# First loads of a second loop, spread over the last eight groups of the loop before it

## What is computed

```python
xn = _layernorm(x, gamma, beta)
x_inner, z = jnp.split(xn @ W_in, 2, axis=-1)
xc = depthwise_conv(x_inner, conv_w, taps=4, causal) + conv_b
x_conv = silu(xc)
xp = x_conv @ W_x                    # B (16), C (16), one delta
delta = softplus(xp[:, :, -1:])
y = selective_scan(x_conv, -exp(A_log), B, C, delta)
y = (y + x_conv * D_skip) * silu(z)
x = _layernorm(x + (y @ W_out + residual))
```

## Time and profile before

| what | us |
|---|---|
| runs, median (lowest to highest of 3) | 1719.43 (1718.05 to 1721.29) |
| the profiled execution, its own time | 1721.67 |
| its span from first to last instruction | 1719.8 |
| first loop and what leads to it, to the end of PE's projections | 0 to 245.6 |
| between the loops and first two steps | 245.6 to 291.1 |
| second loop | 291.1 to 491.5 |
| attention and experts | 491.5 to 1719.8 |
| PE busy over the whole span | 1648.0 |

### The profile page before, as it was taken

One profiled execution on the slowest core, in us unless ns is written; L12 is line 12 of the kernel. 1 busy time (PEld: TensorE's weight loads), 2 busy tenths in 40 slices (PEclk: granted clock), 3 DMA queues, 4 the chain that ended last, 5 costly groups with the idle time before them and its releaser, 6 DMA issues.

```text
span 1719.8 us, 38082 instructions
## 1 busy us (share of the span) xinstructions
PE 1648.0 (96%) x11304; PEld 1492.5 (87%) x11305; DVE 1303.9 (76%) x2688; ACT 947.1 (55%) x1643; POOL 871.4 (51%) x770
## 2 busy tenths in 40 slices
PE   7999986999998999999999998999999999999994
PEld 6777765988987888888888878999999999999994
DVE  6888867888885776776776778767777777777774
ACT  6888876777843334334334345555555565555552
POOL 2111125888972345345345353555666666666664
PEclk9999988999998999999999999999999999999998
DMA  4555556899964343342342344334555455445454
GB/s 151 191 190 190 190 194 203 247 262 265 266 229 140 112 135 103 111 136 97 115 136 100 111 151 122 62 61 98 104 98 106 101 99 114 97 94 117 94 104 106
DMA packets 149263, 240.79 MB, mean 140 GB/s; under 512 B 40960, under 2 KB 104640, under 8 KB 141008
## 3 DMA queue, kind: packets, MB, share of 16 engines
q1 hardware_dynamic: 122608, 203.58, 38.1%
q0 software_dynamic: 26592, 36.46, 12.1%
HBM read 132.30 MB, written 107.68 MB: 140 GB/s over the span
## 4 chain that ended last, share of the span: by engine, by line
PE 62%; DMA 3%; DVE 2%; issue 1%; POOL 1%; ACT 0%; SPq 0%; DVEq 0%; ACTq 0%; POOLq 0%
PE block_banks L3094 22%; PE block_banks L3144 11%; PE block_banks L2976 5%; PE block_banks L2985 5%; PE block_banks L2899 4%; PE block_banks L2998 4%; PE block_banks L2920 2%; PE block_banks L3087 2%; PE block_banks L2939 2%; PE block_banks L2931 2%; PE block_banks L2887 1%; PE block_banks L2956 1%; DMA more<-back_y,back_token 1%; DMA attention_x<-x 1%; POOL sorted L2185 0%
## 5 line engine op out<-in xcount | busy, mean ns | idle before, releaser
L3094 PE MATMUL block_banks<-back_xe_T,back_w_split 128*128 128x256 f32 x3408 | 437.3, 285 | 2.4 <-DVE back_xe_T L2768 1.5
L3094 PEld LDWEIGHTS block_banks<-back_xe_T,back_w_split 128*128 128x128 f32 x3408 | 418.1, 192 | 2.8 <-issue 1.7
L2349 ACT ACTIVATE back_w_split<-back_w_gu 128x1024 fp32r x142 | 149.8, 1056 | 233.3 <-PE block_banks L3094 231.2
L3144 PE MATMUL block_banks<-back_w_down,back_he_T 128*128 x1680 | 213.1, 283 | 1.0 <-DVE back_w_down L2425 1.0
L3144 PEld LDWEIGHTS block_banks<-back_w_down,back_he_T 128*128 128x128 f32 x1680 | 206.6, 192 | 1.2 <-issue 1.2
L2748 DVE TENSOR_TENSOR back_w_split<-back_w_gu,back_w_split 128x1024 fp32r<-128x1024 f32 x142 | 179.6, 1265 | 36.9 <-ACT back_w_split L2349 36.7
L2185 POOL DMA_INDIRECT sorted<-back_x,back_slot x128 | 129.9, 1015 | 127.7 <-DVE back_slot L2571 80.5
L1582 PE MATMUL block_banks<-front_xn_T,front_w_in_parts 128*128 128x512 f32 x768 | 184.8, 395 | 2.4 <-DVE front_xn_T L1353 1.1
L1582 PEld LDWEIGHTS block_banks<-front_xn_T,front_w_in_parts 128*128 128x128 f32 x768 | 141.4, 188 | 39.2 <-DVE front_conv L1346 7.5
L2221 POOL DMA_INDIRECT acc<-back_y,back_token x71 | 112.3, 1581 | 120.5 <-DVE back_y L2787 116.2
L1346 DVE SCALAR_TENSOR_TENSOR front_conv<-block_banks,front_conv_wb,front_conv 128x508 f32<-128x508 f32 (+2 forms) x192 | 140.7, 740 | 33.0 <-ACT front_conv L1130 28.3
(11 more groups left out here) (290 smaller groups left out, 3492.0 us busy)
## 6 DMA issues: line engine op xcount, KB each, us to landing
back_xe<-sorted SPq DMA_DIRECT2D x72, 272.0 KB, 2.8
gate_T<-front_gate_T SPq DMA_DIRECT2D x16, 1024.0 KB, 4.8
xc_T<-front_xc_T SPq DMA_DIRECT2D x16, 1024.0 KB, 5.8
front_xc_in<-xc_T SPq DMA_DIRECT2D x16, 1024.0 KB, 7.4
front_gate_in<-gate_T SPq DMA_DIRECT2D x16, 1024.0 KB, 6.3
front_c_rep<-c_parts SPq DMA_DIRECT2D x128, 64.0 KB, 5.5
front_rows_in<-in_x SPq DMA_DIRECT2D x16, 512.0 KB, 8.2
x<-front_x SPq DMA_DIRECT2D x16, 512.0 KB, 3.1
```

The source lines that it names most:

```text
L2349: nc.scalar.activation(w_split[:, r, 0, m].unsqueeze(1), w_gu[:, bass.ds(e, 1), m], ACT.Copy).then_inc(w_high_ready, 1)
L3094: op = nc.tensor.matmul(dst[:, part, c % 2 * WINDOW:(c % 2 + 1) * WINDOW], w_split[:, r, w_part, m, k * D_FF + c * P:k * D_FF + (c + 1) * ...
L3144: op = nc.tensor.matmul(ps_y[:, s, 0:D_MODEL], he_T[:, r, h_part, k, seq(s)], w_down[:, bass.ds(e, 1), w_part, k], start=(n == 0), stop=(n ...
```

## The change

`load_first` goes. Its 50 DMAs are issued in pieces by `load_sooner(g)`, which SP calls behind the `gate_T` store of each group from 8 to 15. To let it know g as a number, SP's loop runs over groups 2 to 7 only and the last eight groups are written out. Loads of groups 0 and 1 and the data they move stay the same. The wait for all stores becomes a wait for all but the last pair's, and the full wait comes in step 1, ahead of the store of `delta`. No other engine's code changes.

```diff
-            def load_reps(g, u):
-                for c in range(ENDS):
+            def load_reps(g, u, ends=range(ENDS)):
+                for c in ends:
...
-            def load_first(u):
-                if u == 0:
-                    sp.wait_ge(cleared, 3)
-                    sp.wait_ge(chain_step, W_STEPS)
-                sp.wait_ge(xp_stored[u], 16 + 32)
-                load_reps(u, u)
-                load_c(u, u)
-                sp.wait_ge(xc_stored[u], 32)
-                load_xc(u, u)
-                sp.wait_ge(gate_stored[u], 32)
-                load_gate(u, u)
-                load_rows(u, u)
+            def load_sooner(g):
+                if g == GROUPS - 8:
+                    sp.wait_ge(xc_stored[0], 32)
+                    load_xc(0, 0)
+                if g == GROUPS - 7:
+                    sp.wait_ge(gate_stored[0], 32)
+                    load_gate(0, 0)
+                if g == GROUPS - 6:
+                    load_rows(0, 0)
+                    sp.wait_ge(chain_step, W_STEPS)
+                    sp.wait_ge(xp_stored[0], 16 + 32)
+                    load_c(0, 0)
+                if g == GROUPS - 5:
+                    sp.wait_ge(cleared, 3)
+                    load_reps(0, 0, range(ENDS // 2))
+                if g == GROUPS - 4:
+                    load_reps(0, 0, range(ENDS // 2, ENDS))
+                    sp.wait_ge(xc_stored[1], 32)
+                    load_xc(1, 1)
+                if g == GROUPS - 3:
+                    sp.wait_ge(gate_stored[1], 32)
+                    load_gate(1, 1)
+                    load_rows(1, 1)
+                if g == GROUPS - 2:
+                    sp.wait_ge(xp_stored[1], 16 + 32)
+                    load_c(1, 1)
+                if g == GROUPS - 1:
+                    load_reps(1, 1)
...
-                    if last:
-                        load_first(u)
                     sp.wait_ge(gate_T_ready, KI * (g + 1) + 2)
                     sp.dma_start(d["gate_T"][g], gate_T[:, u]).then_inc(gate_stored[u], 16)
-
-            in_pairs(sp, body)
+                    if isinstance(g, int):
+                        load_sooner(g)
+
+            def groups_stored(pairs):
+                for stored, each in ((xc_stored, 16), (gate_stored, 16), (xp_stored, 32)):
+                    for u in range(2):
+                        sp.wait_ge(stored[u], each * pairs + 16)
+
+            body(0, False)
+            with sp.Fori(1, PAIRS - 4) as pair:
+                body(pair, False)
+            for pair in range(PAIRS - 4, PAIRS):
+                body(pair, pair == PAIRS - 1)
             store_xc(GROUPS - 1, 1)
             store_xp(GROUPS - 1, 1)
-            for stored, each in ((xc_stored, 16), (gate_stored, 16), (xp_stored, 32)):
-                for u in range(2):
-                    sp.wait_ge(stored[u], each * PAIRS + 16)
+            groups_stored(PAIRS - 1)
...
                 if is_at(k, 1):
+                    groups_stored(PAIRS)
                     sp.wait_ge(delta_rows_ready, 1)
```

## The result

The changed kernel takes 1725.9 us, median of 8 runs (1722.15 to 1727.64), against 1718.9 us for the kernel before, also 8 runs. The ratio is 1.0037, 95% interval 1.0028 to 1.0046, so about +6.4 us (+4.8 to +7.9); the two medians as they stand lie 7.0 us apart. One run of the kernel before, 3287.91 us, was disturbed and is left out of the ratio. The profiled execution took 1725.78 us, with a span of 1723.9. The forecast was 1719.5, range 1715.5 to 1723.0: the result is outside, on the slow side.

The account below looks back on a forecast made before the run. PE was taken to bound both loops, nearly always busy, with 6.4 us of waits for `xc_in` the most to win. -2.6 + 2.7 = +0.1 us on the median 1719.43 gave 1719.5, range 1715.5 to 1723.0.

Parts of the forecast that it names:

- the sum of what it costs in the first loop: First loop: moved DMAs delay `x_rows` and so PE, 0.7 + 2.0 = +2.7 us, from 1.2 to 4.4.
- g = 8 and 9: First loop: one megabyte each ahead of `x_rows`, 3.4 us, loss 0.37 us each; bounds 0 and 0.94 each.
- g = 10: First loop: nine DMAs ahead, `x_rows` out at 4.7 us, landed at 8.3: covered, 0.2 as upper bound.
- g = 12: First loop: eight small DMAs and the xc load ahead, `x_rows` landed at 11.4 us: loss 2.0, bounds 1.2 to 2.3.
- rival 2: First loop: hole at g = 12 lowers PE's clock, 1.8 us; with dearer queued loads +3.6, 1723.0; chance 0.15.
- g = 11 and 13 to 15: First loop: six small DMAs at the first of these are covered; later stores in the rest cost nothing.
- The term of the gain: Second loop: SP starts sooner, so PE waits less for `xc_in`: -2.6 us, bounds 1.1 and 6.4.
- The wait of 1.11 us: PE's wait for `xc_in` at 291.11, to go since xc of group 2 is issued 8.5 us sooner.
- The lead of 2.6 us at xc of group 4: Second loop: that load goes out at 308.4 instead of 310.99, and SP stays ahead by 2.6 us.
- the waits of 6.4 us to be won: PE's waits for `xc_in`, 5.3 us in the second loop and 1.11 before: the most earlier loads could give back.
- Rival 1: First loop's loads covered, only g = 12 costs, 1.2 us; larger lead, 1716.6, or 1714.2 with all waits won; chance 0.25.
- Rival 3: Second loop: lead lost to transfers ahead in the queue, only 1.11 us come; sum +1.6, 1721.0; chance 0.13.

Follow-up runs that it names:

- e4: Kernel after, with the eight `c_rep` loads of g = 10 cut from 64 KB to 4 KB each, full ones loaded at g = 13; 1721.78 us, one run.
- e7: Kernel after, with only the xc load of g = 12 moved behind the next `x_rows` load; 1724.69 us, one run.
- e11: Kernel after, with the pieces of groups 8 to 11 put behind the `x_rows` load, that of group 12 left ahead; 1728.68 us, one run.
- e5: Kernel before, unchanged, as its second profile; the kernel before against itself measured 0.9997, not assigned to one repeat.
- e9: Kernel after, unchanged, run once more; 1730.31 us against 1722.54 for the kernel before, ratio 1.0040.
- e10: Kernel before, unchanged, as its third profile; the kernel before against itself measured 0.9997, not assigned to one repeat.
- rows first: Kernel after, with every moved piece issued behind the following `x_rows` load; 1717.15 us, 0.9989 of the kernel before; repeated 1719.07 us, 0.9997.
- loads only: Kernel after, with all pieces behind `x_rows` and the full store wait back at the first loop's end; 1717.56 us, 0.9991 of the kernel before.
- e2: Kernel before, with only the wait for the last pair's stores moved to step 1; 1717.52 us, ratio 0.9997; repeated 1721.28 us, 0.9989.

## Why the prediction was wrong, step by step

**The step that failed is the sum of what it costs in the first loop: +2.7 us predicted, 9.2 and 9.9 measured.** Its mechanism was right (`x_rows` late, then DVE's statistics, then the taps, then PE). The terms were too small. One part is common to all: against the kernel before, with PE's own delay so far taken off, the statistics began 0.9, 1.05, 2.95 and 4.05 us later in the four turns, and PE lost 0.3 us less than that (0.2 in the last, the clock apart), where the forecast had 0.48 us of slack. The rest by groups:

- *g = 8 and 9: 0.37 us each predicted.* Measured 0.6 and 0.7. In the kernel after, the load landed 0.87 + 9.0 = 9.87 us behind the store of g = 8, against 6.3 before, so a queued megabyte costs 3.6 us where the forecast took 3.4. That the bracket of PE's hole has 0.32, almost the 0.37, is luck: it leaves out 0.3 us of the loss. SP's timeline at g = 8, and below it the landing from the DMA list of 145 to 156:

```profile
145.72 0.35 SPq L951 DMA_DIRECT2D gate_T<-front_gate_T  x1
146.11 0.43 SPq L889 DMA_DIRECT2D front_xc_in<-xc_T  x1
146.59 0.92 SPq L944 DMA_DIRECT2D front_x_rows<-in_x  x1
...
front_x_rows<-in_x SPq DMA_DIRECT2D x1, 512.0 KB, 9.0
```

- *g = 10: "covered" predicted.* Measured 2.65 us, the term with the largest error against its bound of 0.2. The forecast had the load out at 4.7 us at 0.47 us an issue and landed 3.6 us later. It was out at 5.78 and landed 6.0 us later. It took the landing time of a quiet queue for a load that stands behind half a megabyte each of `rows_in` and `c_rep`. e4 splits the 3.5 us: 1.1 from the issue, 0.7 from what else was in the queue, 1.7 from the data of `c_rep`.
- *g = 12: 2.0 us predicted.* Measured 5.2. The load landed at 13.0 instead of 11.4 us: 1.0 of this is the issue (5.73 against 4.7 us), 0.6 the transfer (7.3 against 6.7). Then 0.2 to 0.3 us for the smaller slack, and 1.36 for the clock, which the sum had at nothing and left to rival 2. e7 shows that the xc megabyte makes this hole, e11 that it needs none of the others.
- *g = 11 and 13 to 15: nothing.* That held.

On the queued megabyte the estimate of 2.4 us came from the Trainium skill ("DMA: Bandwidth & Descriptors", Anatomy of one DMA), whose fit is for single DMAs issued from GpSimd. These are issued from SP and share their queue with stores, and the profile has 3.6 us at g = 8; by the estimate there would have been no hole at g = 8 and 9.

**The term of the gain: -2.6 us predicted.** By the column "between" it is 1.7 us for the two profiles of the kernel after against the three of before (242.2 against 243.8), 2.2 for all nine profiles with the loads moved (241.7), and 4.0 against the profile used. The three of before lie 3.3 us apart, so the size isn't settled. Of the mechanism one part is shown: xc of group 2 was issued at the predicted 276 us plus the first loop's loss. The rest isn't. The wait of 1.11 us is gone, but it's gone in e5 too. The lead of 2.6 us at xc of group 4 isn't there: counted from the end of PE's projections, that load goes out after 63.7 us in the kernel after (318.08 less 254.34) and 63.6 in e9, against 65.4 in the profile used but 63.5 and 63.9 in e5 and e10. So SP's start 8 us sooner is used up by group 4, and the profile used had this load late by chance. And the waits of 6.4 us to be won were in part chance: 3.2 and 3.3 us in the two other profiles of the same kernel.

**Rivals.** Rival 2 comes nearest. The clock fell behind the hole at g = 12 to 0.53, for 1.36 us (1.58 in e9) against its price of 1.8, and its 1723.0 is still below the measured 1725.9: it was priced too low, since its first-loop loss of 4.4 had g = 10 at only 0.2. Rival 1 falls: g = 8 and 9 cost 0.6 and 0.7 us. Rival 3 isn't settled: the waits for `xc_in` shrank to 2.1 and 2.5 us, but only about 1 us of that is less than e5 and e10 had without any change, and the profiles can't tell a gain of 1.1 us from one of 2.6.

**The sum.** 9.2 to 9.9 lost, less 1.7 (mean) to 4.0 (first pair) won, is +5.2 to +8.2 us, and +6.4 and +6.9 were measured. In the first pair of profiles PE is 4.7 us late at the end of the second loop, 496.20 against 491.47, and the execution is 4.1 us longer.

**What stays open.** Between about 990 and 1060 us, far behind both loops, two profiles of one kernel drift apart by up to some 4 us (PE's one wait for DVE's `back_h_low` there is 3.7 us in e5, 2.0 in e10 and 0.8 in the first profile; 0.8 in the kernel after, 3.3 in e9 and 3.8 in e11); what decides it wasn't tried. For that reason, and since their intervals reach 1.0, the versions with rows first (0.9989, 0.9997), loads only (0.9991) and wait only (0.9997, 0.9989) can't be told from the kernel before or from each other. What can be said is that moving the loads behind `x_rows` is 0.4 to 0.5% better than the change as made (1.0037 and 1.0040 over 0.9989 and 0.9997). Over the kernel before it has at most some 0.3%, by the lower ends of the intervals.

## What to carry to other kernels

When DMAs are spread over an in-order queue, put each behind the load whose landing is due first, not ahead of it; the average share of the queue (0.52 here) says nothing on that, only the landing against its due time does. For each DMA ahead count its issue and its data separately, with prices from a stretch with the same traffic: a landing time from a quiet queue was too low here, 3.6 us against 6.0. And take the gain that waits in one profile promise as an upper bound until a second profile of the same kernel shows them too: 6.4 us became 3.2.

## What the runs showed of the hardware that was not expected

- SP's issues aren't of one length. Behind the `gate_T` store, the second and third of the next small DMAs took 0.90 and 1.05 us, the others 0.43; e4 has 0.91 and 1.03 at its g = 11. In e2, where SP goes on behind the last stores without a wait, single small issues took up to 2.35 us. The eight `c_rep` issues took 4.80 us behind the store of g = 10 and 3.70 in the second loop's first step. Their size is not the cause: at 4 KB each they took 4.83.
- Two holes of nearly one length, at the same place in the program, had a different clock behind them: 2.34 us in the kernel after and 2.36 in e9 left it full (24 matmuls in 5.74), 2.26 us in e7 had it low (7.39). PE did the same work ahead of both, with two small holes in each (0.32 and 0.44, 0.40 and 0.57).
- A hole in a run of matmuls costs about 0.3 us more than the idle time in its bracket: 9.09 instead of 8.46 us around one of 0.32. The two pieces of 12 and 24 are shown as 3.01 and 5.75 us, 0.30 more than the 36 in one piece.
